# Second attention of a two-batch transformer: the probability-times-values product in float32, four heads side by side, with the output transposed

## What is computed

```python
q = (x @ q_w.T) as 16 heads of 32;  k, v = (x @ kv_w.T) as 4 groups of 32   # rope on q and k
logits = einsum('bhqd,bhkd->bhqk', q, repeat(k, 4)) / sqrt(32)              # 1024 x 1024 for each head
probs = softmax(where(key > query, -inf, logits))
out = einsum('bhqk,bhkd->bhqd', probs, repeat(v, 4))                        # 1024 x 32 for each head
return out @ c_w.T
```

## Time and profile before

| what | value |
|---|---|
| median of 3 runs | 1522.88 us (1522.76 to 1523.66) |
| profiled execution, its own time | 1512.59 us |
| its span, first to last instruction | 1510.4 us |
| PE busy in the span | 1390.1 us, 92% |
| DVE busy | 1130.6 us, 75% |
| ACT busy | 793.2 us, 53% |
| POOL busy | 891.7 us, 59% |
| mean granted TensorE clock | 0.967 of 2.4 GHz |

### The profile page before, as it was taken

One profiled execution on the slowest core, in us unless ns is written; L12 is line 12 of the kernel. 1 busy time (PEld: TensorE's weight loads), 2 busy tenths in 40 slices (PEclk: granted clock), 3 DMA queues, 4 the chain that ended last, 5 costly groups with the idle time before them and its releaser, 6 DMA issues.

```text
span 1510.4 us, 23389 instructions
## 1 busy us (share of the span) xinstructions
PE 1390.1 (92%) x8445; PEld 1024.2 (68%) x8466; DVE 1130.6 (75%) x2208; ACT 793.2 (53%) x1562; POOL 891.7 (59%) x910
## 2 busy tenths in 40 slices
PE   4988999999888999899899987989999999999996
PEld 3766444444576766678567666868888788878885
DVE  3899556555577999977799996277867767887776
ACT  4654322221326888762588876544545545364442
POOL 1466311213165788854587886676668767865862
PEclk9998999999897999899899999999999999999999
DMA  9000200000064101105601201522323322433310
GB/s 362 15 1 1 70 1 28 1 1 29 1 165 129 44 11 36 57 29 181 168 19 28 44 30 57 195 67 102 112 84 140 111 84 84 156 104 104 112 56 28
DMA packets 42470, 115.01 MB, mean 76 GB/s; under 512 B 2930, under 2 KB 3955, under 8 KB 38772
## 3 DMA queue, kind: packets, MB, share of 16 engines
q1 hardware_dynamic: 41300, 112.21, 22.9%
q10 hardware_dynamic: 1056, 1.31, 0.3%
HBM read 92.28 MB, written 20.97 MB: 75 GB/s over the span
## 4 chain that ended last, share of the span: by engine, by line
PE 44%; DVE 39%; POOL 7%; ACT 5%; issue 3%; DMA 3%; SPq 0%; ACTq 0%; POOLq 0%; DVEq 0%
PE PS L1389 42%; DVE SM L491 9%; DVE cm L479 7%; DVE PH L479 3%; DVE SM L495 2%; POOL PH L1210 2%; PE PS L1398 2%; DVE OO L491 2%; POOL ws_g L1210 1%; DVE OO L479 1%; POOL SM L1210 1%; DVE hm L488 1%; DMA QG<-qs 1%; DVE hm L479 1%; DVE SM L479 1%
## 5 line engine op out<-in xcount | busy, mean ns | idle before, releaser
L1210 POOL TENSOR_TENSOR SM<-SM 128x1 f32<-128x1 f32 x256 | 118.4, 464 | 329.1 <-DVE SM L485 319.0
L1210 POOL TENSOR_TENSOR PH<-EX,PH 128x512 f16<-128x512 f32 (+2 forms) x308 | 277.2, 927 | 51.7 <-DVE PH L715 26.5
L1210 POOL TENSOR_TENSOR ws_g<-rw,ws_g 128x512 fp32r<-128x512 f32 x64 | 138.4, 2162 | 145.8 <-ACT ws_g L877 145.6
L1041 ACT ACTIVATE EX<-PS 128x512 f32<-128x512 f32 (+3 forms) x384 | 187.0, 488 | 55.6 <-PE PS L1389 52.6
L491 DVE TENSOR_REDUCE SM<-PS 128x1 f32<-128x512 f32 (+3 forms) x384 | 191.8, 544 | 20.6 <-PE PS L1389 20.3
L1389 PE MATMUL PS<-VG,PH 128*128 128x97 bf16 x2304 | 167.6, 211 | 22.9 <-DVE OO L479 13.8
L877 ACT ACTIVATE PH<-EX 128x512 f16<-128x512 f32 (+3 forms) x340 | 174.2, 513 | 0.0
L1389 PE MATMUL PS<-KG,QG 96*128 96x512 f32 (+3 forms) x384 | 158.1, 424 | 14.7 <-DMA QG<-qs 11.0
L1389 PE MATMUL PS<-QG,KG 98*128 98x512 f32 (+3 forms) x384 | 166.5, 434 | 0.5 <-ACT EX L1041 0.3
L1389 PEld LDWEIGHTS PS<-VG,PH 128*128 128x128 f16 x2304 | 123.3, 100 | 49.5 <-POOL PH L1210 28.8
L1180 ACT ACTIVATE ab<-hm 128x512 f32<-128x512 f32 x64 | 40.5, 634 | 212.7 <-DVE hm L479 212.7
(11 more groups left out here) (174 smaller groups left out, 3098.3 us busy)
## 6 DMA issues: line engine op xcount, KB each, us to landing
rw<-in_L_ffn_w_gate SPq DMA_DIRECT2D x16, 1024.0 KB, 5.1
rw<-in_L_ffn_w_up SPq DMA_DIRECT2D x16, 1024.0 KB, 5.2
rw<-in_L_ffn_w_down SPq DMA_DIRECT2D x16, 1024.0 KB, 4.8
QG<-qs SPq DMA_DIRECT2D x24, 512.0 KB, 6.7
raw<-in_L_ffn_w SPq DMA_DIRECT2D x3, 2816.0 KB, 19.4
qs<-qm SPq DMA_DIRECT2D x16, 256.0 KB, 8.4
qs<-qn SPq DMA_DIRECT2D x16, 256.0 KB, 8.2
ys<-xA SPq DMA_DIRECT2D x4, 1024.0 KB, 3.9
```

Source lines behind the costliest of these rows:

```text
L1041: e.activation(EX[:, t % 8, 0:W], PS[:, 4 + t % 2, 0:W], ACT.Exp, scale=ISQ, bias=0.0).then_inc(S["ex"], 1)
L1210: return e.tensor_tensor(out, a, b, op)
```

## The change

The second product is turned over. Values are kept as one float32 tile (VG 128 keys x 128, 32 columns for each group), stationary with 32 columns; the float32 exponentials move. The output has value dimension on the partitions and queries on the free axis, so each head needs 32 partitions of a bank; four heads that share values fill bank 6 at partitions 0, 32, 64 and 96. The denominators come from four more matmuls with 32 columns of ones stationary, into bank 7. The order of work becomes group, query half f, key block j, and then the four heads; a step t is four chunks (48 steps for each batch). PH, its splits, the three-part values, the mask matmul of `scores` and the transposes in `project` go. The mask on the exponentials is an `affine_select` on POOL; `drain` (DVE) replaces `take`; maxima have three banks instead of four, scores three instead of two, and `weigh` is run two steps at a time after every eighth chunk. QG is loaded by halves, m_in works on four heads' halves.

```diff
-        VG = at("VG", [128, 8, 4, 98], BF16, 166)
-        EX = at("EX", [128, 8, 512], F32, 52)
-        PH = at("PH", [128, 8, 2, 512], F16, 68)
-        OO = at("OO", [128, 8, 512], F32, 182.25)
+        VG = at("VG", [128, 8, 128], F32, 166)
+        RD = at("RD", [128, 512], F32, 170)
+        EX = at("EX", [128, 16, 512], F32, 52)
+        OO = at("OO", [128, 4, L], F32, 182.25)
...
+        steps3 = [(g, f, j, max(128 * j, 512 * f)) for g in range(4) for f in range(2) for j in range(4 * f + 4)]
+        behind = [[] for _ in range(NS)]
+        for n in range(24):
+            behind[n // 2].append(("m", 24 + n))
+        behind[13].append(("h", 1))
+        for g in range(3):
+            for n in range(48):
+                at_n = 48 * g + 16 + n * 5 // 6
+                behind[at_n].append(("m", 48 * (g + 1) + n))
+                if n == 15:
+                    behind[at_n + 2].append(("h", 2 * (g + 1)))
+            behind[48 * g + 57].append(("h", 2 * (g + 1) + 1))
...
         def top_bank(t):
-            return top_no[t] % 4
+            return top_no[t] % 3
...
+            def drain(b, x):
+                g, f = divmod(x, 2)
+                w.wait_ge(S["oo"], 8 * b + x)
+                w.wait_ge(S["pvd"], 48 * b + 12 * g + (12 if f else 4))
...
+                w.wait_ge(S["dvs"], did(e.reciprocal(RD[:, :], PS[:, 7, :])))
+                tt(OO[:, g, 512 * f:512 * f + 512], PS[:, 6, :], RD[:, :], ALU.mult).then_inc(S["oo"], 1)
...
             def attention(b):
+                for n in range(NS):
+                    for kind, x in behind[n]:
+                        top(b, x) if kind == "m" else shifts(b, x)
+                    if n % 48 == 23:
+                        drain(b, 2 * (n // 48))
+                    if n % 48 == 7 and n > 8:
+                        drain(b, 2 * (n // 48) - 1)
...
+            def exp(b, n):
+                W = width(n // 4)
+                w.wait_ge(S["st"], NS * b + n + 1)
+                w.wait_ge(S["pvd"], max(0, 48 * b + n // 4 - 3))
+                e.activation(EX[:, n % 16, 0:W], PS[:, 3 + n % 3, 0:W], ACT.Exp, scale=ISQ, bias=0.0).then_inc(S["ex"], 1)
...
+                    if diagonal(t):
+                        w.wait_ge(S["ex"], NS * b + n + 1)
+                        p = EX[:, n % 16, 0:128]
+                        e.affine_select(out=p, in_=p, compare_op=ALU.is_ge, fill=0.0, base=0, pattern=[[1, 128]],
+                                        channel_multiplier=-1).then_inc(S["sel"], 1)
...
             def scores(b, n):
+                w.wait_ge(S["ex"], NS * b + max(0, n - 2))
+                mm(PS[:, 3 + n % 3, 0:width(t)], KG[:, g, j * 128:(j + 1) * 128],
+                   QG[:, g % 2, f, a, q0 - 512 * f:512], True, True).then_inc(S["st"], 1)
...
             def weigh(b, t):
+                g, f, j, q0 = steps3[t]
+                w.wait_ge(S["ex"], NS * b + 4 * t + 4)
+                w.wait_ge(S["sel"], diag_to[47] * b + diag_to[t])
                 if j == 0:
+                    w.wait_ge(S["oo"], 8 * b + 2 * g + f)
+                for bank, left in ((6, VG[:, j, g * 32:(g + 1) * 32]), (7, onesf[:, 0:32])):
+                    for a in range(4):
+                        last = mm(PS[32 * a:32 * a + 32, bank, q0 - 512 * f:512], left,
+                                  EX[:, (4 * t + a) % 16, 0:width(t)], j == 0, j == 4 * f + 3, free=True)
                 last.then_inc(S["pvd"], 1)
...
+                for n in range(NS):
+                    scores(b, n)
+                    for kind, x in behind[n]:
+                        maxima(b, x) if kind == "m" else turn_max(b, x)
+                    if n % 8 == 7 and n > 8:
+                        weigh(b, n // 4 - 3)
+                        weigh(b, n // 4 - 2)
+                weigh(b, 46)
+                weigh(b, 47)
...
             def project(b, step):
-                    if k == 0:
-                        w.wait_ge(S["oo"], 32 * b + (31 if i < 4 else 32))
-                        w.wait_ge(S["mxr"], NS * (b + 1))
-                        w.wait_ge(S["ot"], max(0, 8 * b + i - 1))
-                        transpose4(OO[:, i, :], i % 2).then_inc(S["etp"], 1)
```

More of the change, by code:

```diff
@@ L222, in dn_at, with width, diagonal @@
             return 14 * k + j + 1 + (i if j == 10 else 0)
[L225 to L232, removed]
-        NS = 192
[L235 to L241, removed]
+        steps3 = [(g, f, j, max(128 * j, 512 * f)) for g in range(4) for f in range(2) for j in range(4 * f + 4)]
+        units = []
+        for g in range(4):
+            for f in range(2):
+                units += [(g, f, a, i, k0) for a in range(4) for i in range(4 * f, 4 * f + 4) for k0 in range(0, 512 * f + 1, 512)]
+        NS = 192
+        def width(t):
+            return 512 * (steps3[t][1] + 1) - steps3[t][3]
+        def diagonal(t):
+            return steps3[t][3] == 128 * steps3[t][2]
+        diag_to = [4 * sum(diagonal(x) for x in range(t + 1)) for t in range(48)]
+        early = [[("m", 2 * v), ("m", 2 * v + 1)] for v in range(8)] + [[("h", 0)] + [("m", n) for n in range(16, 24)]]
+        behind = [[] for _ in range(NS)]
[9 more added lines that the diff above has]
+            behind[48 * g + 57].append(("h", 2 * (g + 1) + 1))
+        tops = [t for v in early + behind for t in v]
         top_no = {t: n for n, t in enumerate(tops)}
         def top_bank(t):
-            return top_no[t] % 4
+            return top_no[t] % 3
         fours, slots4 = [], []
@@ L375, in sp_program @@
                     q_out(0, qm, tb)
-                for piece in range(3):
-                    q_in(0, piece)
+                q_in(0)
                 for tb in range(2):
@@ L731, in project @@
+                drain(b, 7)
             def project(b, step):
@@ L1295, in attention @@
-            def attention(b):
-                for step in range(10):
-                    values(b, step)
-                for t in range(NS + 8):
-                    x = t - 3
-                    if 0 <= x < NS and not lo_on_dve(x):
-                        W = chunks[x % 12][2] - chunks[x % 12][1]
-                        if hi_on_dve(x):
-                            w.wait_ge(S["hiv"], n_hi[True][NS] * b + n_hi[True][x + 1])
-                        else:
-                            w.wait_ge(S["hia"], n_hi[False][NS] * b + n_hi[False][x + 1])
-                        tt(PH[:, x % 8, 1, 0:W], EX[:, x % 8, 0:W], PH[:, x % 8, 0, 0:W], ALU.subtract).then_inc(
-                            S["lop"], 1)
-                    if b == 1 and t in (157, 163, 169, 175):
-                        i = (t - 157) // 6
+            def attention(b):
+                for n in range(NS):
+                    t = n // 4
+                    if diagonal(t):
[3 more added lines that the diff above has]
+                                        channel_multiplier=-1).then_inc(S["sel"], 1)
+                    if b == 1 and n in (157, 163, 169, 175):
+                        i = (n - 157) // 6
@@ L1648, in attention @@
                     last.then_inc(S["vj"], 1)
-                for step in range(8):
-                    values(b, step)
-                    for n in range(3 * step, 3 * step + 3):
-                        if n == 13:
-                            turn_max(b, 0)
-                        maxima(b, n)
-                for t in range(NS + 8):
-                    if t < NS:
-                        scores(b, t)
-                    if t + LEAD < NS:
-                        maxima(b, t + LEAD)
-                    if 0 <= t - 6 < NS:
-                        weigh(b, t - 6)
-                    if (t + 11) % 12 == 0 and (t + 11) // 12 < 16:
-                        turn_max(b, (t + 11) // 12)
+                for v, events in enumerate(early):
+                    if v < 8:
+                        values(b, v)
+                    for kind, x in events:
+                        maxima(b, x) if kind == "m" else turn_max(b, x)
+                for n in range(NS):
+                    scores(b, n)
+                    for kind, x in behind[n]:
+                        maxima(b, x) if kind == "m" else turn_max(b, x)
+                    if n % 8 == 7 and n > 8:
[3 more added lines that the diff above has]
+                weigh(b, 47)
             def project(b, step):
```

301 lines of the change are left out of this document (98 added, 203 removed).

## The result

The changed kernel takes 1586.09 us (median of 4 runs, 1584.11 to 1588.47) against 1523.24 for the kernel before (1522.76 to 1523.66): ratio 1.0413, 95% interval 1.0395 to 1.0431. It is slower, as forecast, but by 63 us and not by 143. Some 9 of the 72 us are there because the profiled execution of before (1512.59 us) ran 10 us under its own median.

A forecast was written before the change was run, and what follows sets the result against it. DVE was taken to bound the loops, PE under 3 us behind. (120 + 132.5 + 4) x 2 = 513, less 369.1 and 1.0, is +143: 1655.6 profiled, 1666 us median; range 1505 to 1945.

The forecast's parts named there:

- 576 units of the product: Second product in `weigh`, in pieces of 512 moving columns, 288 a batch: 0.46 us each, 132.5 us a batch.
- rest of the loops, tile changes in it: Attention loops outside the second product: 120 us a batch from blocks of work, plus 4 for changing tiles.
- edges: Projection, loop ends and loop starts: 7.0 us saved, +3.0 twice, 0 for the starts; together 1.0 less.
- the overlap in the unit's price: Second product: one head's second record overlaps only the next head's first, so 512 columns cost 0.46 us, not 0.92.
- four tiles at once: Rival for the second product: all four column tiles overlap, 0.23 us per 512 columns, +10, 1533 us; chance 0.27.
- 4.4 and 7.6 us in its block: Second and fourth of six blocks in a steady group: lengths set by `drain` on DVE, 4.4 and 7.6 us.
- The change of tiles: PE going from whole array to quarter tiles and back, 48 times a batch: 0 to 8 us, taken as 4.
- `m_in` now stands behind six more loads ...: 0: Loop start, SP's queue: six more QG loads ahead are issued while DVE still reduces, so they cost 0.
- 16 x 0.44 = 7.0 us: `project`: four transposes dropped for each tile of 128 queries, 0.44 us each tile, saving 7.0 us.
- the +3.0: Loop end: reciprocal, multiply and subtract before the first projection, 4.9 us instead of 1.9, so +3.0 twice.
- The rest can move it by 20 us or so: Whole forecast: the price of 512 product columns decides; all other terms together shift the time by about 20 us.
- The side: Direction of the whole change: slower, chance 0.79, against faster 0.18 and same 0.03.

The follow-up runs named there:

- e1: The changed kernel with all four heads' products written to partitions 0 to 31, one tile (output not the attention's): 1951.27 us.
- e2: The changed kernel with the four heads' products on two column tiles, partitions 0 to 31 and 32 to 63 (output not the attention's): 1694.24 us.
- e3: The changed kernel with the drain's 128x512 reciprocal replaced by a copy (output multiplied, not divided): 1508.18 us, ratio 0.9923.
- e6: The changed kernel with 14 unread float32r products of 512 columns added at two places of each group, 98 a batch: 1558.01 us, ratio 1.0225.
- e4: The changed kernel with the second group's QG loads behind the first shifts in SP's queue instead of ahead: 1574.85 us, ratio 1.0358.
- e12: The changed kernel with the output projection in banks 0 to 3 in turn instead of 2 and 3: 1585.19 us, ratio 1.0437.
- e17: The changed kernel with shifts before QG loads, drain on ACT, DVE and POOL, projection's add on DVE, second reciprocal at chunk 13, not 7: 1509.16 us, ratio 0.9920.
- e5: The changed kernel with the drain split: ACT copies banks 6 and 7 out, DVE takes the reciprocal later, POOL multiplies: 1527.70 us, ratio 1.0031.

## Why the prediction was wrong in size

| term, both batches, us | forecast | measured | difference |
|---|---|---|---|
| 576 units of the product | 265 | 576 x 0.215 = 124 | -141 |
| rest of the loops, tile changes in it | 248 | 423.7 - 124 = 300 | +52 |
| edges | -1 | 4.6 + 5.9 + 6.9 = 17.4 | +18 |
| against 369.1 before | +143 | +72 | -71 |

**The step that failed** is the overlap in the unit's price: "So at most those two overlap: a unit costs 0.46 us". e1 and e2 show that all four tiles stream side by side. The unit alone at 0.86 stands close to my 0.92 (four passes at the 0.230 of a stream that holds weight loads of 128 columns too). The order of issue doesn't keep the tiles from overlapping: the two records of a head stand ahead of the next head's in e2 and in the changed kernel as well. The rule of the Trainium skill that I gave the smaller chance ("TensorEngine Tiling (Array Packing)", Theoretical Speedup, up to 4 times for 32 columns) is the one that the trace bears out: 3.43 / 0.86 = 4.0.

**The rival "four tiles at once"** was therefore the true mechanism, and gave 1533 with 1509 to 1559. It too misses, by 53 us, for a reason that no case of mine had.

**The term left out** is the clock. I charged each drain with the wait it makes, 4.4 and 7.6 us in its block, but every matmul at the full clock. The waits were about right: the second block of the group shown takes 4.4 us from one `weigh` to the next (537.28 to 541.72), the fourth 10.8 (553.62 to 564.40), of which the last 6 at the lower level. With e3's busy time in place of its own, a loop would take 211.9 - 19.5 = 192.4 us; less the 62 of the product that is 130 for the rest of a batch, where I had 124. The other 19.5 us a batch are the clock, 39 of the 52 in the table's second line. e6 shows it is the clock and not a wait counted twice. The kernel before stands 19.0 us in its first loop as well, so the sum of the waits is no larger than it was.

**Reciprocal and selects** were as worked out: 3.36 us where 3.5 was forecast from two small rows, the drain 4.1 against 4.2, the select 0.294 us and hidden. The records came out at 1536, two for each matmul. The change of tiles costs some 0.1 us each way: the 14 products of a fill take 3.41 us when `weigh` follows (536.81 to 540.22) and 3.30 when a score does, and the last four heads ahead of a score take 0.97 us and not 0.86. With 24 blocks a batch that is about 5 us, an estimate from these rows, where I had 4.

**Edges**, three steps, each wrong. "`m_in` now stands behind six more loads ...: 0" cost two waits, 5.57 and 6.33 us; e4 took both away, and the first scores of the two loops start 5.3 and 11.2 us earlier. "16 x 0.44 = 7.0 us" for the transposes was mostly not there to gain. In the second batch POOL paced the steady tiles, and one of its instructions grew by 0.48 us. In the first batch the tiles went from 3.62 us apart to 3.41, where the two banks held them (e12), so seven tiles gave 1.0 us. And at a loop's end the +3.0 was seen (from the last product to the first projection 5.1 us against 1.9, and 4.9 against 2.4 at the second), but PE stands in it, and the first projection then took 4.82 and 4.93 us from start to start and not 2.85.

**The side** was right for the wrong sum, which is luck: two terms too small by 70 us beside one too large by 141. "The rest can move it by 20 us or so" was the weakest sentence; the rest moved it by 70.

e3 came out 17 us under the lower end of what was expected for it. Its span is 77.4 us shorter than the changed kernel's: 29 us are standstill in the loops (30 expected), 39 the clock there (at most as much again expected), and 10 lie outside the loops, which the expectation had left out; at the loops' ends the waits fell from 4.4 and 4.9 us to 1.7 and 2.2.

What stays open: how much the clock takes from the kernel before and from e17 in their loops (0.95 and 0.98, 0.92 and 0.91) was not measured, nor what about the waits lowers the clock: their length, their number in a stretch, or what stands around them.

## What to carry to other kernels

Four float32 matmuls of 32 stationary columns, put on the four column tiles, took together here what one of them takes alone (0.86 us for 512 columns); that made the product cheap enough to drop a whole splitting scheme, though the loops came out no shorter than with it (368.2 us in e17, 369.1 before). Before an engine's work is turned over, look at what the receiving side does between PE's blocks: a single instruction of 3.4 us there was paid as a wait and again as slow matmuls, and what helped (e5) was to free PSUM with two short copies and do the long work later. Work taken off PE gains only where the chain of another engine, here POOL's full timeline, isn't already the pace; and a change of operand from PSUM to SBUF can slow an instruction of another engine that the diff leaves as it was.

## What the runs showed of the hardware beyond that

- Adding 23 us of matmuls to each batch made the kernel 28 us faster (e6): clock of the first loop 0.83 to 0.95.
- The kernel before stands 19.0 us in its first loop, in waits of at most 1.8 us, at a clock of 0.95, the changed one 19.0 us, in waits of up to 3.1 us, at 0.83.
- Going from the whole array to column tiles of 32 and back took some 0.1 us each way (3.41 against 3.30 us, 0.97 against 0.86).
- POOL's power over 128x512 takes 81.9 us, DVE's reciprocal of the same 3.36, 6.5 ns a column.
- DVE's subtract with both inputs in SBUF lengthens a POOL add that starts behind it from 1.30 to 1.78 us (its own 0.69 stays); where the add starts first, the add keeps its 1.29 us and the subtract takes up to 1.37.
